# Tile 0's squares to SBUF, tile 7's low parts to GpSimd, and two scans and three loads moved back

## The chip, the cores and the metric

One core of one Trainium2 chip runs the whole kernel. The metric is the device time in microseconds, of which the median of the runs counts. TensorE multiplies matrices, VectorE (DVE in the profile) and ScalarE (ACT) do elementwise work, GpSimd (POOL) does a little of it and issues some transfers, and SyncE (SP) only issues transfers.

## The reference, cut to what matters

Four layers, each added to its input: x (4 sequences of 1024 tokens, 512 features) goes through

```python
x = x + L0(x)   # gelu(x @ fc1) @ [shared fc2, expert fc2 chosen per sequence]
x = x + L1(x)   # a 512x512 matrix chosen per sequence; its result is x2
ctx = ema(x2, tau_ctx)                            # h = alpha*h + b, along the tokens
gated = x2 * sigmoid([x2, ctx] @ Wg + bg)
mod = 0.5 + sigmoid(gelu(x2 @ Wn1 + bn1) @ Wn2 + bn2)           # 4 rows per token
temporal = sum_d blend[d] * ema(gated * mod[d], tau[d])         # 4 scans per feature
out = (gelu(x2 @ Wsoma) * sigmoid(temporal @ Wtemp)) @ Wout
x3 = x2 + layernorm(out) * gamma + beta
x = x3 + L3(x3)  # a 512x512 matrix chosen per sequence
```

All in float32. The layernorm needs the sum over the 512 features of the squares of out.

## The kernel before

A tile is 512 tokens; there are eight (NT), two to a sequence, and LAST is tile 7. Each of the four 128-row chunks of a tile is called c or m. A float32 product is made of three passes over a high part (rounded by ScalarE) and a low part (what is left, a subtraction): hi*hi, hi*lo and lo*hi. So nearly every operand passes through ScalarE (`..._hi`) and then a `low_part` (`..._lo`).

Up to about 760 us the first two layers run. Then comes the third, in rounds r over the tiles: round r makes n1(r) and mo(r) (the modulation rows), gate(r, m), te(r-1, m) (temporal product), l3(r-2, m) (the last layer), ou(r-1, m) (output product), so(r, m) and so_pair(r) (soma products), and ss(r-1) (the sum of squares over partitions). Every engine's order is written out by hand, and semaphores hold the engines together. An engine waits in its own order, so what stands behind a waiting instruction waits too.

The names that matter here:
- `o_of(i, m)` on ScalarE copies the output product out of its bank and squares it; `square_of` says where a square goes, which for tile 0 is the bank itself. `sum_squares(i)` on VectorE adds the four squares to `sumsq`, and counts in s_ssq. `ss(i)` multiplies `sumsq` with ones, and `rows_std(i)` makes 1/std of it.
- x2 of tile 7: `x2_hi`, `x2_lo`, and then its store to x2hl_dram. x2's halves come back as `x2_slot`, by `load_slot(i, c)`; slots 2 and 3 of the next tile are free only when so_pair has used chunks 0 and 1 (s_x2free).
- ctx: `context(t, c)` on VectorE is a scan in x_raw; `ctx_hi(t, c)` (two copies on ScalarE) and `context_lo(t, c)` split it, and `store_ctx(t, h)` stores two chunks.
- `load_xt(i, h)` brings x2 of tile i for `gated_of`. xt of tile 2 lies where x_raw of tile 7 lies (168 KiB), so it waits for all stores of contexts. `load_l3w(b)` brings the last layer's weights of a sequence; every l3(i, m) waits for all four chunks.
- VectorE makes a chunk of temporal out of `gated_of`, and four times `drive_of`, `trace_of` (the scan) and `add_of`; these go by the names traces_a to traces_d, first_traces and first_sum. `temporal_low(i, p)` splits two chunks.

These waits carry the order around the change:

```python
elif i == 2:                                             # load_xt
    on.wait_ge(s_ctxst, 16 * HALVES * NT)
...
on.wait_ge(s_xt[i % 3], 16 * HALVES * (i // 3 + 1))      # gated_of
...
elif i < LAST:                                           # so_pair
    on.wait_ge(s_ssq, SH * i)
...
on.wait_ge(s_h1hi, mo_split_no(i))                       # mo, tiles from 3 on
on.wait_ge(s_h1lo, mo_split_no(i))
```

Of the kernel before, what the change touches and what calls it, by code (L numbers as in the profile page):

```python
# [5 lines left out]
F32 = mybir.dt.float32  # L6
F32R = mybir.dt.float32r
# [36 lines left out]
def build(nc, x, tok16, tok8, small, fc1_w, fc2_w, exp_w, exp_b, l1_w, l1_b, wg, wn1, wsoma, wtemp, wout,  # L44
# [16 lines left out]
    with ctx:  # L61
# [3 lines left out]
        def place(name, kib, shape, dt=F32):  # L65
            return nc.alloc_sbuf_tensor_at(name, [P] + shape, dt, offset=base + int(kib * KIB))
# [84 lines left out]
        x3_hi_late = place("x3_hi_late", 68, [KC, TOK], F32R)  # L151
        sq_late = place("sq_late", 40, [SH, TOK])
        spikes_hi_late = place("spikes_hi_late", 112, [KC, TOK], F32R)
        y_sb = [place("y_sb0", 94, [TOK]), place("y_sb1", 4, [TOK])]

        idx = const("idx", 2 * B, I32)
# [309 lines left out]
        def te_bank(m):  # L466
            return bank[m]
# [44 lines left out]
        def square_of(i, m):  # L512
            if i == LAST:
                return last_squares[m][:, :]
            return te_bank(m)[:, :] if i < LAST - 1 else sq_late[:, m - 1, :]


# [13 lines left out]
        def _(eng):  # L531
# [207 lines left out]
            def load_l3w(b):  # L739
                for c in range(KC):  # L740
                    if b == B - 1 and c == KC - 1:
                        on.wait_ge(s_pe["SO"], KC * LAST)
                    elif b == B - 1:
                        on.wait_ge(s_pe["WG"], KC * LAST + 3)
                    elif b:
                        on.wait_ge(s_pe["L3"], KC * HALVES * b)
                    elif c < 2:
                        for q in range(KC):
                            on.wait_ge(s_hl7[q], 16)
                    else:  # L750
                        on.wait_ge(s_fc2, UNITS)

                        on.wait_ge(s_stlo, STAGED)
                        on.wait_ge(s_pstlo, 16 * len(PARKED))
                        for row in range(2):
                            on.wait_ge(s_hbst[row], 16 * K8 * PAIRS)
                    eng.dma_start(l3w_of_tile(HALVES * b, c)[:, :, :].bitcast(F32), parked("L3", KC * b + c)).then_inc(s_l3w[c], 16)
# [128 lines left out]
            load_slot(2, 0)  # L886
            load_slot(2, 1)
            store_ctx(LAST, 0)
            store_ctx(LAST, 1)
            load_xt(2, 0)  # L890
            load_xt(2, 1)
            load_l3w(0)

            for r in range(1, NT + 2):
                if 1 < r < LAST:
                    load_slot(r + 1, 0)
                    load_slot(r + 1, 1)
                if r >= 2:
                    i = r - 2
                    if r == LAST:  # L900
                        load_l3w(B - 1)
                    for m in range(KC):
                        on.wait_ge(s_y, KC * i + m + 1)
                        source = y_sb[m % 2][:, :] if i < LAST else temporal[:, m, :]
                        eng.dma_start(out[i, :, m, :], source).then_inc(s_out[m % 2], 16)
                    if i + 3 < NT:
                        load_xt(i + 3, 0)
                        load_xt(i + 3, 1)
                    if i % HALVES and i < LAST - 2:
                        load_l3w((i + 1) // HALVES)  # L910
                if r + 1 < NT:
                    for c in range(KC):
                        load_ctx(r + 1, c)
                    load_slot(r + 1, 2)
                    load_slot(r + 1, 3)
            for s in range(2):
                on.wait_ge(s_out[s], 16 * HALVES * NT)
            on.wait_ge(s_x2st, 16 * NT)
# [6 lines left out]
        def _(eng):  # L925
# [60 lines left out]
            for c in range(KC):  # L986
                on.wait_ge(s_fc2, HC * LAST + (9, 11, 12, 13)[c])
                store_hl(LAST - 1, c)
            on.wait_ge(s_made, len(MADE))
            eng.memset(wn2_hl[:, :, :].bitcast(F32), 0.0).then_inc(s_wn2, 1)  # L990
            for i in range(HALVES, NT, HALVES):
                last_columns(i)
        @block.scalar
        def _(eng):
# [479 lines left out]
            ctx_hi(LAST, 1)  # L1474
            wg_tanh(1, 2)
            q_of(1, 3)
            ctx_hi(LAST, 2)
            ctx_hi(LAST, 3)
            wg_tanh(1, 3)
            for m in range(KC):  # L1480
                o_of(0, m)
# [3 lines left out]
            soma_of(1, 1)  # L1485
            for m in range(SH):
                temporal_hi(1, m)
            rows_std(0)
            soma_of(1, 2)
            soma_of(1, 3)  # L1490

            for r in range(2, NT):
                if r == 2:
                    h1_of(r)
                    temporal_hi(r - 1, 3)
                else:
                    temporal_hi(r - 1, 3)
                    h1_of(r)
                    h1_hi_of(r)
                mod_of(r)  # L1500
                modulation_out(r)
                modulation_back(r)
                q_of(r, 0)
                wg_tanh(r, 0)
                te_tanh(r - 1, 0)
                for m in range(HALVES):
                    x3_hi_of(r - 2, m)
                te_tanh(r - 1, 1)
                for m in range(HALVES, KC):
                    x3_hi_of(r - 2, m)  # L1510
                te_tanh(r - 1, 2)
                te_tanh(r - 1, 3)
                for m in range(SH):
                    spikes_hi(r - 1, m)
                q_of(r, 1)
                spikes_hi(r - 1, SH)
                wg_tanh(r, 1)
                q_of(r, 2)
                y_of(r - 2, 0)
                y_of(r - 2, 1)  # L1520
                if r < LAST:
                    y_of(r - 2, 2)
                    y_of(r - 2, 3)
                wg_tanh(r, 2)
                q_of(r, 3)
                o_of(r - 1, 0)
                o_of(r - 1, 1)
                wg_tanh(r, 3)
                o_of(r - 1, 2)
                o_of(r - 1, 3)  # L1530
                if r <= LAST - 1:
                    sumsq_hi(r - 1)
                soma_of(r, 0)
                soma_of(r, 1)
                for m in range(SH):
                    temporal_hi(r, m)
                if r < LAST:
                    rows_std(r - 1)
                soma_of(r, 2)
                soma_of(r, 3)  # L1540
# [31 lines left out]
        def _(eng):  # L1572
# [283 lines left out]
            def so_pair(i):  # L1856
                if i == 0:
                    on.wait_ge(s_x1, KC * NT)
                elif i < LAST:
                    on.wait_ge(s_ssq, SH * i)  # L1860
                else:
                    on.wait_ge(s_sq, KC * i)
                for c in range(KC):
                    for m in (2, 3):
                        mm = so_part(i, m, c)
                        if c == KC - 1:
                            mm.then_inc(s_pe["SO"], 1)
                    if c < 2:
                        mm.then_inc(s_x2free, 1)
# [124 lines left out]
            for r in range(1, NT):  # L1994
                if r > 1:
                    n1(r)
                    gate(r, 0)
                for m in range(SH):
                    te(r - 1, m)
                if r == 1:  # L2000
                    gate(r, 1)
                te(r - 1, SH)
                if r > 1:
                    gate(r, 1)
                gate(r, 2)
                if r > 1:
                    for m in range(KC if r < LAST else 2):
                        l3(r - 2, m)
                gate(r, 3)
                for m in range(KC):  # L2010
                    ou(r - 1, m)
                so(r, 0)
                so(r, 1)
                if r < LAST:
                    ss(r - 1)
                so_pair(r)

            l3(LAST - 2, 2)
            l3(LAST - 2, 3, range(2))
# [20 lines left out]
        def _(eng):  # L2040
# [574 lines left out]
            x2_of(LAST, 3)  # L2615
            traces_a(1, 0)
            spikes(0, 0)
            for c in range(KC):
                x2_lo(LAST, c)
            spikes(0, 1)  # L2620
            first_traces(1, 0)
            context(LAST, 0)
            context(LAST, 1)
            spikes(0, 2)
            gate_sum(1, 1)
            context(LAST, 2)
            context(LAST, 3)
            spikes(0, 3)
            first_sum(1, 0)
            spikes_low(0, 0, 2)  # L2630
            spikes_low(0, 2, 2)
            gate_sum(1, 2)
            traces_c(1, 0)
            context_lo(LAST, 0)
            context_lo(LAST, 1)
            traces_d(1, 0)
            gate_sum(1, 3)
            context_lo(LAST, 2)
            context_lo(LAST, 3)
            traces_a(1, 1)  # L2640
            traces_b(1, 1)
            traces_c(1, 1)
# [12 lines left out]
            low_part(wn2_hl[:, 1, 0:TAUS], wn2_sb, wn2_hl[:, 0, 0:TAUS]).then_inc(s_wn2, 1)  # L2655
            temporal_low(1, 0)
            temporal_low(1, 2)
            for r in range(2, NT):
                if r > 2:
                    h1_low(r)  # L2660
# [2 lines left out]
                gate_sum(r, 0)  # L2663
                for m in range(KC):
                    x3_of(r - 2, m)
                traces_a(r, 0)
                spikes(r - 1, 0)
                spikes(r - 1, 1)
                x3_low(r - 2, 0, 2)
                x3_low(r - 2, 2, 2)  # L2670
                spikes(r - 1, 2)
                first_traces(r, 0)
                spikes(r - 1, 3)
# [118 lines left out]
```

## Time and profile before

| | |
|---|---|
| median of 3 runs | 1296.02 us (1295.71 to 1296.36) |
| the profiled execution | 1295.54 us, its span 1293.7 us |
| mean granted clock of TensorE | 0.997 |
| TensorE matmuls busy | 1274.4 us, 99% |
| VectorE busy | 1066.6 us, 82% |
| ScalarE busy | 718.7 us, 56% |
| GpSimd busy | 66.8 us, 5% |
| DMA | 262.62 MB, mean 203 GB/s |

Times of rows are in microseconds from the start of the span. The busy share is a mean over the whole kernel; what an edit is worth is read at its place. The span is from the first to the last instruction of the profiled execution, and the time of that execution is 1.8 us more.

### The profile page before, as it was taken

The numbers are of one execution on the slowest core, as the hardware profiler recorded it, in microseconds if no ns is written. First come the engines' busy times: TensorE is split into PE (matmuls) and PEld (weight loads), VectorE is DVE, ScalarE is ACT, GpSimd is POOL, SyncE is SP. The second block draws the span as 40 slices with busy tenths as digits, with TensorE's granted clock in tenths as the row PEclk, the third lists the DMA queues.
The fourth block names the chain that finished last, engine by engine and source line by source line (L and its number), as shares of the span: only waits on it lengthen the run. The fifth ranks groups of instructions, "written<-read, shape, count | busy, mean of one in ns | idle before, by whom it ended". The sixth has DMA issues, their size and how long they took to land.

```text
span 1293.7 us, 17500 instructions
## 1 busy us (share of the span) xinstructions
PE 1274.4 (99%) x6109; PEld 1068.1 (83%) x6109; DVE 1066.6 (82%) x1698; ACT 718.7 (56%) x1369; POOL 66.8 (5%) x102
## 2 busy tenths in 40 slices
PE   9999999999999999999999999899999999999998
PEld 7788888888888888888887888778888888888867
DVE  7877777887786987777875899999898989898974
ACT  6576465776565875566763353443636363636254
POOL 0010000000000000000000000002000210021000
PEclk9999999999999999999999999999999999999999
DMA  8357653658744657645558797966465646663301
GB/s 293 98 171 238 192 174 122 220 174 270 216 170 145 238 167 266 225 141 178 188 206 277 297 329 289 345 227 231 160 240 215 227 164 232 224 222 137 130 17 65
DMA packets 114286, 262.62 MB, mean 203 GB/s; under 512 B 10344, under 2 KB 32872, under 8 KB 109080
## 3 DMA queue, kind: packets, MB, share of 16 engines
q1 hardware_dynamic: 94336, 183.27, 41.6%
q10 hardware_dynamic: 15032, 62.45, 13.7%
q0 software_dynamic: 4832, 15.79, 3.2%
q8 instruction: 49, 0.80, 0.3%
q14 instruction: 37, 0.30, 0.1%
HBM read 181.19 MB, written 80.28 MB: 202 GB/s over the span
## 4 chain that ended last, share of the span: by engine, by line
PE 81%; DVE 13%; DMA 2%; ACT 2%; issue 2%; ACTq 0%; DVEq 0%
PE bank L1577 27%; PE bank L1578 27%; PE bank L1579 26%; DVE drive L2289 4%; DVE drive L2278 2%; DVE temporal L2305 1%; DMA x_slot<-x2hl_dram 1%; DMA hb_in<-hb_dram 1%; DVE x_hl L2044 1%; DVE h_hl L2044 1%; DVE w_hl L2044 1%; DVE t_lo L2044 0%; DVE x_raw L2244 0%; DVE gated L2265 0%; DMA x_raw<-in_x 0%
## 5 line engine op out<-in xcount | busy, mean ns | idle before, releaser
L1577 PE MATMUL bank<-h_hl,w_hl 128*128 128x512 f32 x512 | 199.6, 390 | 0.0
L1578 PE MATMUL bank<-h_hl,w_hl 128*128 128x512 f32 x512 | 199.3, 389 | 0.0
L1579 PE MATMUL bank<-h_hl,w_hl 128*128 128x512 f32 x512 | 199.2, 389 | 0.0
L1577 PE MATMUL bank<-t_hi,sp_hl 128*128 128x512 f32 x448 | 175.2, 391 | 3.5 <-DVE t_lo L2044 1.1
L1578 PE MATMUL bank<-t_lo,sp_hl 128*128 128x512 f32 x448 | 174.4, 389 | 0.0
L1579 PE MATMUL bank<-t_hi,sp_hl 128*128 128x512 f32 x448 | 174.4, 389 | 0.0
L1577 PEld LDWEIGHTS bank<-h_hl,w_hl 128*128 128x128 f32 x512 | 96.1, 188 | 21.1 <-issue 1.3
L1579 PEld LDWEIGHTS bank<-h_hl,w_hl 128*128 128x128 f32 x512 | 96.1, 188 | 20.0
L1578 PEld LDWEIGHTS bank<-h_hl,w_hl 128*128 128x128 f32 x512 | 96.2, 188 | 19.6
L1577 PEld LDWEIGHTS bank<-t_hi,sp_hl 128*128 128x128 f32 x448 | 84.1, 188 | 24.3 <-issue 1.8
L1579 PEld LDWEIGHTS bank<-t_hi,sp_hl 128*128 128x128 f32 x448 | 84.1, 188 | 17.5
L1578 PEld LDWEIGHTS bank<-t_lo,sp_hl 128*128 128x128 f32 x448 | 84.1, 188 | 17.1
L2278 DVE SCALAR_TENSOR_TENSOR drive<-gated,small_sb,mod_t 128x512 f32<-128x512 f32 x128 | 92.6, 744 | 2.7
L2044 DVE TENSOR_TENSOR w_hl<-w_raw,w_hl 128x512 fp32r<-128x512 f32 x128 | 86.4, 683 | 4.4 <-ACT w_hl L1035 3.9
L1102 ACT ACTIVATE h_hl<-hb_in 128x512 fp32r<-128x512 f32 x64 | 40.1, 627 | 82.2 <-DMA hb_in<-hb_dram 63.3
L1035 ACT ACTIVATE w_hl<-w_raw 128x512 fp32r<-128x512 f32 x128 | 78.3, 619 | 6.4 <-PE bank L1579 6.3
L2289 DVE TENSOR_TENSOR_SCAN drive<-alpha,trace_last,drive 128x512 f32<-128x512 f32 x64 | 80.2, 1274 | 0.5
L2044 DVE TENSOR_TENSOR h_hl<-hb_in,h_hl 128x512 fp32r<-128x512 f32 x64 | 43.8, 684 | 42.9 <-ACT h_hl L1102 42.9
L2289 DVE TENSOR_TENSOR_SCAN drive<-alpha,drive 128x512 f32<-128x512 f32 x64 | 76.7, 1214 | 0.5
L1577 PE MATMUL bank<-x_slot,wg_hl 128*128 128x256 f32 x256 | 73.0, 285 | 0.0
L1578 PE MATMUL bank<-x_slot,wg_hl 128*128 128x256 f32 x256 | 73.0, 285 | 0.0
L1579 PE MATMUL bank<-x_slot,wg_hl 128*128 128x256 f32 x256 | 73.0, 285 | 0.0
(229 smaller groups left out, 3026.8 us busy)
## 6 DMA issues: line engine op xcount, KB each, us to landing
wg_hl<-wg_dram ACTq DMA_DIRECT2D x24, 1536.0 KB, 7.8
fc_raw<-in_fc_w SPq DMA_DIRECT2D x32, 512.0 KB, 4.2
hb_dram<-hb_out SPq DMA_DIRECT2D x64, 256.0 KB, 2.2
hb_in<-hb_dram ACTq DMA_DIRECT2D x64, 256.0 KB, 4.2
x2hl_dram<-x_hl POOLq DMA_DIRECT2D x28, 512.0 KB, 5.6
x_slot<-x2hl_dram SPq DMA_DIRECT2D x26, 512.0 KB, 5.8
wg_hl<-wg_dram SPq DMA_DIRECT2D x8, 1536.0 KB, 8.5
stage<-in_l_w SPq DMA_DIRECT2D x32, 256.0 KB, 3.4
```

The source lines that it names most:

```text
L1035: eng.activation(w2_hl[v % 3][:, 0, :, :], w2_raw[:, j, :, :], ACT.Copy).then_inc(s_w2hi, 1)
L1102: eng.activation(h_hl[v % 4][:, 0, :], hb_in[v % 4][:, :], ACT.Copy).then_inc(s_hhi, 1)
L1577: eng.matmul(ps, w_hi, x_hi, start=first, stop=False, skip_group_check=resumed)
L1578: eng.matmul(ps, w_hi, x_lo, start=False, stop=False, skip_group_check=resumed)
L1579: return eng.matmul(ps, w_lo, x_hi, start=False, stop=final, skip_group_check=resumed)
L2044: return eng.tensor_tensor(lo, raw, hi.bitcast(F32), ALU.subtract)
L2278: eng.scalar_tensor_tensor(drive[d % 2][:, :], gated[:, :], blend_sb[:, TAUS * c + d:TAUS * c + d + 1], mod_t[:, d, :], ALU.mult, ALU.mult ...
L2289: eng.tensor_tensor_scan(traced, alpha[:, 1 + d:2 + d].to_broadcast([P, TOK]), traced, start, ALU.mult, ALU.add).then_inc(s_trace, 1)
L2305: eng.tensor_tensor(temporal[:, c, :], drive[d % 2][:, :], temporal[:, c, :] if d > 1 else drive[0][:, :], ALU.add).then_inc(s_add, 1)
```

## The change

It has five parts. The squares 1 to 3 of tile 0 go to three places in SBUF (200, 202 and 90 KiB) instead of their banks; chunks 2 and 3 of the last layer's weights, which lie over them, wait for the sum. With the banks free sooner, so_pair(1) waits for the squares alone, and ss(0) goes behind it. The subtractions x2_lo and context_lo of tile 7 go from VectorE to GpSimd. The scans of tile 7's chunks 2 and 3 go behind tile 1's temporal_low, their ctx_hi on ScalarE behind the modulation rows of round 2. In SyncE's queue the second store of tile 7's context, and with it the loads of xt(2) and of the last layer's weights, go behind the loads of ctx(2) and slots (2, 2) and (2, 3). On ScalarE rows_std(0) goes behind two somas, and on VectorE traces_a(2, 0) behind two spikes and the low parts of x3.

```diff
+        sq_first = [place(f"sq_first{m}", at, [TOK]) for m, at in enumerate((200, 202, 90))]
...
             if i == LAST:
                 return last_squares[m][:, :]
+            if i == 0:
+                return sq_first[m - 1][:, :]
...
                         on.wait_ge(s_pstlo, 16 * len(PARKED))
+
+                        on.wait_ge(s_ssq, SH)
...
             store_ctx(LAST, 0)
-            store_ctx(LAST, 1)
-            load_xt(2, 0)
-            load_xt(2, 1)
-            load_l3w(0)
...
                     load_slot(r + 1, 2)
                     load_slot(r + 1, 3)
+                if r == 1:
+                    store_ctx(LAST, 1)
+                    load_xt(2, 0)
+                    load_xt(2, 1)
+                    load_l3w(0)
...
+            for c in range(KC):
+                on.wait_ge(s_x2hi, KC * LAST + c + 1)
+                eng.tensor_tensor(halves(x_hl[:, 1, c, :]), even_odd(x_raw[LAST % 2][:, c, :]),
+                                  halves(x_hl[:, 0, c, :]).bitcast(F32), ALU.subtract).then_inc(s_x2lo, 1)
             on.wait_ge(s_made, len(MADE))
             eng.memset(wn2_hl[:, :, :].bitcast(F32), 0.0).then_inc(s_wn2, 1)
+            for c in range(KC):
+                on.wait_ge(s_ctxhi, KC * LAST + c + 1)
+                z = x_raw[LAST % 2][:, c, :]
+                eng.tensor_tensor(z[:, 0:PAIR].bitcast(F32R), z[:, 0:PAIR], z[:, PAIR:], ALU.subtract
+                                  ).then_inc(s_ctxlo, 1)
...
             q_of(1, 3)
-            ctx_hi(LAST, 2)
-            ctx_hi(LAST, 3)
             wg_tanh(1, 3)
...
-            rows_std(0)
             soma_of(1, 2)
             soma_of(1, 3)
+            rows_std(0)
...
                 modulation_back(r)
+                if r == 2:
+                    ctx_hi(LAST, 2)
+                    ctx_hi(LAST, 3)
                 q_of(r, 0)
...
             def so_pair(i):
-                elif i < LAST:
+                elif 1 < i < LAST:
                     on.wait_ge(s_ssq, SH * i)
...
-                if r < LAST:
+                if 1 < r < LAST:
                     ss(r - 1)
                 so_pair(r)
+                if r == 1:
+                    ss(0)
...
             spikes(0, 0)
-            for c in range(KC):
-                x2_lo(LAST, c)
             spikes(0, 1)
...
-            context(LAST, 2)
-            context(LAST, 3)
             spikes(0, 3)
...
-            context_lo(LAST, 0)
-            context_lo(LAST, 1)
             traces_d(1, 0)
             gate_sum(1, 3)
-            context_lo(LAST, 2)
-            context_lo(LAST, 3)
             traces_a(1, 1)
...
             temporal_low(1, 0)
             temporal_low(1, 2)
+            context(LAST, 2)
+            context(LAST, 3)
...
-                traces_a(r, 0)
+                if r > 2:
+                    traces_a(r, 0)
                 spikes(r - 1, 0)
                 spikes(r - 1, 1)
                 x3_low(r - 2, 0, 2)
                 x3_low(r - 2, 2, 2)
+                if r == 2:
+                    traces_a(r, 0)
```

## Rows read from the trace of the kernel before

**Rows 1.** The page's busy times (us, share of the span, instructions).

```profile
PE 1274.4 (99%) x6109; PEld 1068.1 (83%) x6109; DVE 1066.6 (82%) x1698; ACT 718.7 (56%) x1369; POOL 66.8 (5%) x102
```

**Rows 2.** TensorE's waits, 800 to 1000 us: total, times, longest.

```profile
PE bank L1885 <- DVE sumsq L2359: 3.9, 1, 3.9
PE bank L1577 <- DMA x_slot<-x2hl_dram: 2.7, 1, 2.7
```

**Rows 3.** One window: length, busy time by engine, PEclk, DMA share, GB/s.

```profile
852.00:854.00 2.00, 2.00 (x9) 1.71 (x8) 2.00 (x3) 0.73 (x1) 0.00 (x0) 0.53 0.30 119
```

**Rows 4.** SyncE's timeline: start, length, line, transfer, count.

```profile
834.58 0.79 SPq L702 DMA_DIRECT2D xt<-x_dram  x2
...
842.76 0.32 SPq L728 DMA_DIRECT2D x_slot<-x2hl_dram  x1
```

**Rows 5.** DMA issues at 912.6, 652.4, all, 834.6, 891.1, 837.1 us: count, KB, us to landing.

```profile
x_slot<-x2hl_dram SPq DMA_DIRECT2D x1, 512.0 KB, 4.5
...
ctx_dram<-x_raw SPq DMA_DIRECT2D x2, 512.0 KB, 3.4
...
ctx_dram<-x_raw SPq DMA_DIRECT2D x16, 512.0 KB, 6.1
...
xt<-x_dram SPq DMA_DIRECT2D x2, 512.0 KB, 4.7
...
xt<-x_dram SPq DMA_DIRECT2D x2, 512.0 KB, 9.0
...
l3w_hl<-l3w_dram SPq DMA_DIRECT2D x2, 512.0 KB, 9.3
```

**Rows 6.** VectorE's timeline: start, length of all, instruction, count, wait before it.

```profile
810.27 0.66 DVE L2346 SCALAR_TENSOR_TENSOR soma<-bank,soma 128x512 f32<-128x512 f32 x1
...
817.62 0.75 DVE L2044 TENSOR_TENSOR x_raw<-x_raw 128x256 fp32r<-128x256 f32 x2
...
836.33 2.25 DVE L2359 TENSOR_TENSOR sumsq<-bank,sumsq 128x512 f32<-128x512 f32 x3
...
854.86 2.35 DVE L2044 TENSOR_TENSOR temporal_lo<-temporal,ts_hi 128x1024 fp32r<-128x1024 f32 x2
...
864.40 0.68 DVE L2265 SCALAR_TENSOR_TENSOR gated<-bank,xt 128x512 f32<-128x512 f32 x1
...
877.30 0.69 DVE L2257 TENSOR_TENSOR bank<-bank,q_sb 128x512 f32<-128x512 f32 x1
...
906.51 0.69 DVE L2359 TENSOR_TENSOR sumsq<-bank,sumsq 128x512 f32<-128x512 f32 x1 [1.46 <-ACT bank L1251]
...
920.80 0.69 DVE L2044 TENSOR_TENSOR h_lo<-h,h_hi 128x512 fp32r<-128x512 f32 x1 [0.48 <-ACT h_hi L1149]
```

**Rows 7.** ScalarE's timeline, from 808 to 861 us.

```profile
808.61 0.65 ACT L1204 ACTIVATE bank<-bank,small_sb 128x512 f32<-128x512 f32 x1
...
833.68 0.58 ACT L1251 ACTIVATE bank<-bank 128x512 f32<-128x512 f32 x1
...
845.14 1.28 ACT L1264 ACT_TABLE_LOAD   x1
...
856.54 0.68 ACT L1153 ACTIVATE mod_row<-bank,small_sb 4x512 f32<-4x512 f32 x1 [1.00 <-PE bank L1735]
...
860.29 0.38 ACT L1177 ACTIVATE q_sb<-bank 128x256 f32<-128x256 f32 x1 [2.32 <-DMA mod_dram<-mod_row]
```

**Rows 8.** TensorE's timeline: so(1, 1)'s last, gate(2, 0), l3(0, 0), mo(3).

```profile
834.42 0.39 PE L1579 MATMUL bank<-x_slot,wsoma_hl 128*128 128x512 f32 x1
...
852.79 0.41 PE L1577 MATMUL bank<-x_slot,wg_hl 128*128 128x256 f32 x1
...
878.94 0.40 PE L1577 MATMUL bank<-x_hi,l3w_hl 128*128 128x512 f32 x1
...
922.05 0.39 PE L1577 MATMUL bank<-h_hi,wn_hl 128*64 128x512 f32 x1
```

**Rows 9.** GpSimd's copies (min/median/max ns) and its affine_select (busy us, mean ns).

```profile
L971 POOL COPY trace_last<-drive x48: 182/707/1035, 871.8 to 1177.3; 128x1 f32<-128x1 f32 x48
...
L932 POOL TENSOR_SCALAR_AFFINE_SELECT ident<-ident 128x128 f32<-128x128 f32 x1 | 0.3, 282 | 0.2 <-POOL ident L930 0.2
```

## The prediction

> **What bounds the kernel now.** I read the page first: TensorE is busy in 1274.4 of 1293.7 us [rows 1], so all that any edit can win is what TensorE waits, plus what its clock takes back. The waits of TensorE between 800 and 1000 us come second. Nearly all of it is two waits: 3.9 us for tile 0's sum of squares and 2.7 us for a half of x2 on its way from DRAM [rows 2]. The windows give the third part: from 852 us the granted clock is 0.53 [rows 3], which is the lower of the two levels (1.2 of 2.4 GHz) after the second wait; a 256-column matmul then costs 0.21 instead of 0.12 us, about 1.6 us in all, and some 0.8 us more after the first wait. Tile 1's first two soma products end at 834.65, and gate(2, 0) begins at 852.79 [rows 8]; the work between them is 9.15 us (24 + 12 matmuls of 0.227 and 0.95 for ss), so 9.0 us need not be there. Then I went to what releases each wait: SyncE's queue [rows 4], the landing times [rows 5], VectorE [rows 6] and ScalarE [rows 7], and followed them as far as the next round, because VectorE hardly idles there: from 862 to 921 us it waits only 1.46 us ahead of 906.5 and 0.48 ahead of 920.8 [rows 6].
>
> **Removed waits.** With ss(0) behind so_pair(1), TensorE goes on at 834.65: the pair needs only the fourth square, which ends at 833.68 + 0.58 = 834.3 [rows 7]. Writing the squares to SBUF instead of a bank I cost at nothing; 0.1 us each, which no row suggests, would just be hidden. The pair's 24 matmuls of 0.227 end at 840.1. The sum of squares ended at 836.33 + 2.25 = 838.6 [rows 6] and comes sooner below, so the 3.9 us go. The pair's sixth matmul now ends at 836.0, not 842.7, and so does SyncE's wait for a free slot [rows 4]. In front of that load nothing is queued any more (the 1 MB of xt and the 2 MB of l3w stood there), so 4.5 us as in the next round [rows 5] is nearer than its 8.0 here: landed at 840.7, wanted at 840.1 + 1.0 (ss) + 1.4 = 842.4. The 2.7 us go too. n1(2) ends at 843.8.
>
> **VectorE.** It loses x2_low (2.4 us), two scans (2.4) and four context_low (two pairs of 0.67 [rows 6]); 6.1 us. Most of that turns into a wait: spikes(0, 3) cannot start before te_tanh(0, 3) ends at 808.61 + 0.66 = 809.3 [rows 7], 0.95 before its 810.27 [rows 6]. Behind it only the two pairs are gone, so it is 0.95 + 1.34 = 2.3 ahead; I take 2.1 for a little friction with GpSimd. The sum of squares then ends at 836.5, and temporal_low(1, ·), 854.86 + 2.35, ends at 855.0 instead of 857.15.
>
> **GpSimd.** The trace shows no 128x512 subtraction on it. Near rows: affine_select of 128x128 in 0.28 us, times four 1.1, and a copy of one column that can last 1.0 instead of 0.2 [rows 9]; so 1.1 to 2.1 us each. I take 1.2, near the row of like width, and 0.6 to 0.75 for 256 columns. x2's four then end at about 803 and the store of x2 is issued only at 807.2 anyway: 2.1 us each, done by 804.5, would still be hidden. The first two context_lo end at 815, before their store can matter.
>
> **What TensorE finds next.** ScalarE: temporal_hi(1, 2) at 842.4, then 0.63, 1.3 for two somas, 0.7 for rows_std and 0.7 for h1 with a table load of 1.28 [rows 7] ahead of each of the last two: h1 of tile 2 is there at 848.3. TensorE is at mo(2) at 845.2: 3.1 us of a new wait, and probably a low clock behind it. te(1, 0) needs temporal_low(1, 0), at 854.0; before, it began at 859.4. So of 9.0 us, 5.4 are left; four te and two gates later gate(2, 2) ends at 873.5 instead of 878.94 [rows 8].
>
> **The loads behind the moved scans.** xt of tile 2 lies where x_raw of tile 7 lies: load_xt(2) waits until all of tile 7's context is stored (s_ctxst), and load_l3w(0) is queued behind it. Before, xt was issued at 834.58 [rows 4], l3w right behind. Now: the two scans on VectorE 855.0 to 857.4; on ScalarE ctx_hi(7, 2) and (7, 3) stand behind mod_of(2) and the way of its rows to DRAM and back, where q_of(2, 0) stood. From mod_of to q_of it was 860.29 - 856.54 = 3.75 [rows 7]; mod_of now begins at 853.4, behind temporal_hi(1, 3), so they begin at 857.2, and four copies of 0.4 end at 858.8; context_lo(7, 3) on GpSimd ends at 859.5 to 860.5; store at 860.2. The store takes 3.4 us alone and 6.1 as the median [rows 5]; wg(10), 1.5 MB, runs beside it, so 5.0: 865.3. The two halves of xt take 4.7 us with nothing beside, 9.0 with a wg started 1 us before [rows 5]; here that wg is nearly done: 6.0 after the second issue at 865.8. So xt(2) is there at X = 871.7 (ends: 868.4 and 876).
>
> gated_of(2, 0) waits for it; before it ran at 864.40 [rows 6]. The diff puts two spikes and two x3_low (3.47 us) ahead of it, but they are done by 867. From gated_of to gate_sum(2, 1) it was 877.30 - 864.40 = 12.90 us [rows 6], now 12.90 - 3.47 = 9.43: gate_sum(2, 1) at X + 9.43, late by L = X - 867.87 = 3.8 us. Behind it VectorE has no gap until 906.5, then 1.46 and 0.48 [rows 6]. h1_low(3) ended at 921.45 and mo(3) began at 922.05 [rows 8], 0.6 of slack. So mo(3) moves by L - 1.46 - 0.48 - 0.6 = X - 870.4 = **+1.3 us**. Behind mo(3) hang the modulation rows, q and the gates of tile 3, where VectorE had a gap of over 3 us; so the shift is neither won back nor grows.
>
> The other branch: the last l3w needed 9.3 us from issue [rows 5]; issued at 866.3 to 867.9, with the rest of a wg and two slot loads about, all four are there at 877.5 to 878.5. TensorE is ready at 873.5, waits 4 us or so, and pays up to 1.7 us of low clock: l3(0, 2) at -0.4 to +1.2 against before. y_of(0, 0), behind gate_sum(2, 1) on ScalarE, gives about the same. The VectorE branch is the later one, and sets.
>
> **Sum.** 9.0 us won by 853, 5.4 by the first te, about 1 at l3(0, 0), -1.3 at mo(3): 1295.54 + 1.3 = 1296.8 for the profiled execution; the median of the three runs is 0.5 above that execution, so **1297.3**. The reordered SyncE queue otherwise costs nothing: ctx_slot is loaded sooner, slots (3, 0) and (3, 1) wanted at 916 are issued at 869, the output stores start after 882. GpSimd's last_columns(2) stands behind context_lo(7, 3) at 860.5, its first scan after 872.
>
> **Rivals.** (1) *Forecast*: the late xt(2) eats the gain, -2.6 to +2.6 us; 0.48. (2) *Faster*: store and load take no more than they do on an empty queue, or less (rows say 3.4 + 4.7, X = 868.4, which gives -2.0); at X of 866.9 VectorE never waits and L is -1.0. mo(3) is then 3.5 us sooner: 1292.5. Against it: a wg is always in flight there. With what I may have missed in my own chain, 0.20. (3) *Slower by late transfers*: store 6.1 and xt 8 give X = 874.8, mo(3) +4.4: 1300.4. It decides from X = 873.0 on. The low clock after a wait of 4 us speaks for it on TensorE's side; 0.19. (4) *Slower by the lock*: GpSimd's copies of one column take 182 ns at best, 707 in the middle and 1035 at most [rows 9], so something beside them holds them up; the same may hold VectorE up. If each GpSimd subtraction stops VectorE for its length, 4 x 1.1 us less a gap of 2.8 before spikes(0, 3), and 2 x 0.6 behind it, make 2.8 us where I put 0.2: temporal_low, and X with it, 2.6 later, +3.9: 1299.9; 0.13. The Trainium skill, SBUF — State Buffer ("Who interferes with whom"), has that rule: a VectorE instruction with two SBUF inputs and a GpSimd one that reads SBUF exclude each other for the whole instruction. The row agrees for GpSimd's side; none shows VectorE held.
>
> **How the numbers follow.** 0.2% is 2.6 us, about what can be told from no change. Faster: (2), 0.20. Same: (1), 0.48. Slower: (3) and (4), 0.32. The range goes down to a little under rival 2, 1292.0, and up past rival 3 but not to the far end of X (876 gives +5.6), 1301.5.
>
> **What would show it.** No wait at ss(0) nor at n1(2) near 840; mo(2) near 848 after some 3 us of wait; te(1, 0) near 854; VectorE idle for about 4 us ahead of gated_of(2, 0), released by xt's load, at 871.7; TensorE waiting for l3w ahead of l3(0, 0) near 878; a lower clock once or twice between 845 and 882; mo(3) near 923. If gated_of(2, 0) doesn't wait, the forecast is wrong and the kernel is some 3 us faster; if GpSimd's pieces take 2 us and VectorE's scans beside them grow beyond 1.3, it is rival 4.

## The result, and the profile after

The changed kernel takes **1300.2 us** (median of 7 runs, 1299.4 to 1302.8) where the kernel before takes 1295.4 (7 runs, 1294.2 to 1296.4): ratio 1.004, 95% interval 1.003 to 1.005. It is 4.8 us slower, more than the 2.6 us that can be told from no change. The range of 1292.0 to 1301.5 holds it; the likeliest case, +1.3 us, is not what came. What came has the price of rival 3, 1300.4.

The profiled execution took 1301.53 us. One caution for every table below: it already ran 1.47 us behind the kernel before when tile 1's soma products began (830.68 against 829.21 us), and the executions of one kernel differ by some 3 us, so positions in the span are compared after taking this offset off. I call that *aligned*.

The page, answering to [rows 1]: TensorE's work has grown by 0.8 us, its span by 5.9.

```profile
span 1299.6 us, 17499 instructions
...
PE 1275.2 (98%) x6109; PEld 1067.8 (82%) x6109; DVE 1067.9 (82%) x1690; ACT 718.7 (55%) x1369; POOL 78.6 (6%) x110
```

TensorE's waits from 800 to 1000 us, answering to [rows 2]:

```profile
PE bank L1595 <- DMA l3w_hl<-l3w_dram: 5.3, 1, 5.3
PE bank L1753 <- ACT h L1160: 3.4, 1, 3.4
...
PE bank L1595 <- DVE h_lo L2064: 0.8, 1, 0.8
PE bank L1595 <- DVE temporal_lo L2064: 0.2, 1, 0.2
```

Both old waits are gone and two new ones add up to more: 3.4 us for h of tile 2, 5.3 us for the last layer's weights. TensorE's timeline shows where they stand; brackets hold the wait and its releaser.

```profile
841.57 1.02 PE L1903 MATMUL bank<-sumsq,ones 128*128 128x512 f32 x2
842.02 0.80 PE L1595 MATMUL bank<-x_slot,wn_hl 128*128 128x512 f32 x1
...
850.16 1.33 PE L1753 MATMUL bank<-h,small_sb 128*4 128x512 f32 x2 [3.38 <-ACT h L1160]
...
855.96 0.47 PE L1595 MATMUL bank<-ts_hi,wtemp_hl 128*128 128x512 f32 x1 [0.20 <-DVE temporal_lo L2064]
...
881.11 0.77 PE L1595 MATMUL bank<-x_hi,l3w_hl 128*128 128x512 f32 x1 [5.33 <-DMA l3w_hl<-l3w_dram]
```

ss(0) and n1(2) follow the soma products without a gap. Aligned, te(1, 0) starts at 854.5 against 859.4, so 4.9 us are in hand; l3(0, 0) starts at 879.6 against 878.9 [rows 8], so 0.7 us is owed; mo(3), at 927.36, starts 3.8 us late. The whole loss lies between 855 and 927.

VectorE's timeline tells the rest of it, answering to [rows 6]:

```profile
854.60 2.35 DVE L2064 TENSOR_TENSOR temporal_lo<-temporal,ts_hi 128x1024 fp32r<-128x1024 f32 x2
856.87 2.46 DVE L2264 TENSOR_TENSOR_SCAN x_raw<-alpha,g_last,x_raw 128x512 f32<-128x512 f32 x2
...
867.29 2.34 DVE L2064 TENSOR_TENSOR x_lo<-xt,x_hi 128x1024 fp32r<-128x1024 f32 x2
875.48 0.69 DVE L2285 SCALAR_TENSOR_TENSOR gated<-bank,xt 128x512 f32<-128x512 f32 x1 [5.85 <-DMA xt<-x_dram]
...
884.93 0.69 DVE L2277 TENSOR_TENSOR bank<-bank,q_sb 128x512 f32<-128x512 f32 x1
...
911.22 2.27 DVE L2379 TENSOR_TENSOR sumsq<-bank,sumsq 128x512 f32<-128x512 f32 x3
```

The engine that had hardly a gap up to 906 us stands still for 5.85 us, waiting for xt of tile 2. The gap ahead of the sum of squares (1.46 us in [rows 6]) is used up. SyncE's timeline, and then the transfers' time to landing (count, KB, us), say why xt is late:

```profile
862.40 0.32 SPq L693 DMA_DIRECT2D ctx_dram<-x_raw  x1
869.58 0.80 SPq L706 DMA_DIRECT2D xt<-x_dram  x2
870.55 2.32 SPq L763 DMA_DIRECT2D l3w_hl<-l3w_dram  x4
```

```profile
ctx_dram<-x_raw SPq DMA_DIRECT2D x1, 512.0 KB, 7.2
...
xt<-x_dram SPq DMA_DIRECT2D x2, 512.0 KB, 4.7
...
l3w_hl<-l3w_dram SPq DMA_DIRECT2D x4, 512.0 KB, 7.5
```

The store waits for the moved scans, takes 7.2 us, and the loads of xt and of the weights wait for the store. xt was issued at 834.58 before [rows 4], at 869.58 now. Windows of the same stretch (length, busy time by engine, granted clock, DMA share, GB/s), answering to [rows 3]:

```profile
850.00:855.00 5.00, 4.84 (x22) 3.67 (x23) 4.93 (x8) 0.47 (x2) 0.00 (x0) 0.66 0.00 0
875.00:880.00 5.00, 0.78 (x7) 0.58 (x5) 4.48 (x6) 1.27 (x3) 0.58 (x1) 0.81 1.05 402
880.00:885.00 5.00, 3.89 (x9) 3.12 (x10) 4.86 (x8) 0.63 (x1) 1.26 (x3) 0.51 1.01 372
```

The granted clock falls behind the first wait and already within the second: 0.66 and 0.81 are means over both levels, 0.51 is the lower one (1.2 of 2.4 GHz). From l3(0, 0) to gate(2, 3) it is 12.76 us instead of 10.91: 1.85 us for the clock.

### The profile page after: what moved, and what is told of

Read it like the earlier page. It is cut to its first block and busy times, and to the rows that moved or that the text cites. A ratio compares the mean times of both kernels' runs of the same rounds, so it can differ in the third digit from the quotient of the medians.

```text
span 1299.6 us, 17499 instructions
## 1 busy us (share of the span) xinstructions
PE 1275.2 (98%) x6109; PEld 1067.8 (82%) x6109; DVE 1067.9 (82%) x1690; ACT 718.7 (55%) x1369; POOL 78.6 (6%) x110
## 5 line engine op out<-in xcount | busy, mean ns | idle before, releaser
L1205 ACT ACTIVATE bank<-bank,small_sb 128x512 f32<-128x512 f32 x32 | 21.2, 661 | 98.3 <-DVE bank L2277 98.3
L1595 PE MATMUL bank<-x_slot,wg_hl 128*128 128x256 f32 x256 | 72.5, 283 | 0.0
L1596 PE MATMUL bank<-x_slot,wg_hl 128*128 128x256 f32 x256 | 72.4, 283 | 0.0
```

The lines of the kernel that those rows point to most:

```text
L1205: eng.activation(ps[:, :], ps[:, :], ACT.Tanh, bias=bg_sb[:, m:m + 1], scale=0.5).then_inc(s_wgt, 1)
L1595: eng.matmul(ps, w_hi, x_hi, start=first, stop=False, skip_group_check=resumed)
L1596: eng.matmul(ps, w_hi, x_lo, start=False, stop=False, skip_group_check=resumed)
```

## The experiments

Eight kernels, each with 5 to 11 runs beside 15 to 21 runs of the kernel before on the same chip. "After" is the changed kernel, "before" the one without it; names are those of the kernel section above.

| kernel | median us | ratio to before, 95% | mo(3), aligned, against before |
|---|---|---|---|
| changed kernel | 1300.2 | 1.004 (1.003 to 1.005) | +3.8 |
| 1 scans back | 1293.56 | 0.9991 (0.9982 to 1.0000) | -2.3 |
| 2 low parts back | 1299.65 | 1.0039 (1.0025 to 1.0053) | +3.9 |
| 3 weights first | 1300.57 | 1.0042 (1.0029 to 1.0056) | +4.5 |
| 4 squares and queue | 1293.37 | 0.9990 (0.9981 to 0.9999) | -2.7 |
| 5 squares alone | 1295.43 | 1.0001 (0.9992 to 1.0010) | -0.9 |
| 6 scans moved alone | 1300.15 | 1.0038 (1.0025 to 1.0052) | +4.0 |
| 7 contexts on GpSimd | 1293.51 | 0.9986 (0.9977 to 0.9995) | -2.7 |
| 8 queue alone | 1296.36 | 1.0010 (1.0001 to 1.0019) | -0.4 |

The last column is the start of mo(3) counted from the start of tile 1's soma products, less the same distance before (922.05 - 829.21 = 92.84 us).

**1. The moved scans back.** From the changed kernel:

```diff
             gate_sum(1, 1)
+            context(LAST, 2)
+            context(LAST, 3)
             spikes(0, 3)
...
             temporal_low(1, 2)
-            context(LAST, 2)
-            context(LAST, 3)
```

with ctx_hi(7, 2) and (7, 3) and traces_a(2, 0) back in their old places too.

> The changed kernel with the two scans of tile 7's chunks 2 and 3, their ctx_hi and traces_a(2, 0) back where they stood before; squares, ss order, GpSimd's low parts and SyncE's new order stay. Theory (late loads: xt(2) and the weights come too late because the store waits for the moved scans): the store is issued near 839, xt(2) is there by 846, neither VectorE nor TensorE waits for either, and the total falls to 1292.5 (1291 to 1294.5). Rival (GpSimd's lock on VectorE is what costs): the lock on x2's four pieces and on context_lo is still there, so the total stays at 1297 to 1300.

Measured: 1293.56 us, within what the first theory gave, and 6.6 us below the changed kernel's median (6.2 us when each is set against the kernel before on its own chip: +4.8 and -1.4). TensorE's waits have only one entry over 1 us, and VectorE's row at gate_sum(2, 0) has no wait worth the name:

```profile
PE bank L1752 <- ACT h L1160: 5.3, 1, 5.3
```

```profile
859.96 0.70 DVE L2276 TENSOR_TENSOR bank<-bank,q_sb 128x512 f32<-128x512 f32 x1 [0.16 <-ACT q_sb L1195]
```

What follows: with the scans back, xt and the weights are never late, and the loss is gone (0.9991, 0.9982 to 1.0000). The GpSimd parts are all still in it, so the lock rival's 1297 to 1300 did not come.

**2. The low parts back on VectorE.** From the changed kernel: the two loops on GpSimd go, x2_lo(LAST, 0 to 3) stands behind spikes(0, 0) again, and context_lo(LAST, 0) to (LAST, 3) run on VectorE, the last two behind the moved scans.

```diff
-            for c in range(KC):
-                on.wait_ge(s_x2hi, KC * LAST + c + 1)
...
             spikes(0, 0)
+            for c in range(KC):
+                x2_lo(LAST, c)
...
+                if r == 2:
+                    context_lo(LAST, 2)
+                    context_lo(LAST, 3)
                 gate_sum(r, 0)
```

> The changed kernel with x2_lo and context_lo of tile 7 back on VectorE (the last two behind z_of of round 2, since the scans stay moved). Late loads: the store is issued 0 to 1.5 us sooner, everything behind it is hardly changed: 1299.3 (1298 to 1300.5). Lock rival: the 4.8 us come back, 1296 or less.

Measured: 1299.65 us. The lock, rival 4, falls as the cause of the loss: with no GpSimd arithmetic in the kernel the loss is the same, and so is the wait.

```profile
873.81 0.69 DVE L2276 SCALAR_TENSOR_TENSOR gated<-bank,xt 128x512 f32<-128x512 f32 x1 [5.87 <-DMA xt<-x_dram]
```

**3. The weights ahead of the store.** From the changed kernel:

```diff
                 if r == 1:
+                    load_l3w(0)
                     store_ctx(LAST, 1)
                     load_xt(2, 0)
                     load_xt(2, 1)
-                    load_l3w(0)
```

> The changed kernel with load_l3w(0) ahead of store_ctx(7, 1) and load_xt(2) in SyncE's queue. TensorE no longer waits 5.3 us ahead of l3(0, 0) nor pays for the low clock behind it. If VectorE's late gated_of(2, 0) sets the end, as the prediction had it, mo(3) stays where it is within 1 us: 1299.5. If TensorE's wait for the weights and its low clock set it, 2 to 4 us come back: 1297.

Measured: 1300.57 us. TensorE's 5.3 us wait for the weights is gone, and nothing is won: another wait stands behind it.

```profile
PE bank L1595 <- ACT y_sb L1301: 6.1, 1, 6.1
PE bank L1753 <- ACT h L1160: 3.6, 1, 3.6
```

l3(0, 2) needs y_of(0, 0), which stands behind gate_sum(2, 1) on ScalarE's path, and that hangs on xt. So the weights alone are worth nothing: with them in time, TensorE stands still for xt by another way. Reading only TensorE's waits would have named the weights. That VectorE's branch is the later one at mo(3) is shown by the changed kernel's own wait there, 0.8 us for h_lo. In experiment 3 mo(3) begins without a wait, 0.7 us later still: aligned, l3(0, 2) starts at 886.0 and not at 887.0, but it starts at the low clock behind its wait of 6.1 us, and gate(2, 3) starts at 894.0 and not at 892.4.

**4. Squares and queue only.** From the kernel before, these edits and no other:

```diff
+        sq_first = [place(f"sq_first{m}", at, [TOK]) for m, at in enumerate((200, 202, 90))]
...
+            if i == 0:
+                return sq_first[m - 1][:, :]
...
+                        on.wait_ge(s_ssq, SH)
...
             store_ctx(LAST, 0)
-            store_ctx(LAST, 1)
-            load_xt(2, 0)
-            load_xt(2, 1)
-            load_l3w(0)
...
+                if r == 1:
+                    store_ctx(LAST, 1)
+                    load_xt(2, 0)
+                    load_xt(2, 1)
+                    load_l3w(0)
...
-                elif i < LAST:
+                elif 1 < i < LAST:
...
-                if r < LAST:
+                if 1 < r < LAST:
                     ss(r - 1)
                 so_pair(r)
+                if r == 1:
+                    ss(0)
```

> The kernel before with only the squares in SBUF, ss(0) behind so_pair(1) and SyncE's new order; scans, low parts, rows_std and traces_a(2, 0) stay as before. Late loads: both waits at 835 to 851 go, the store is issued at 838, nothing waits for xt(2): te(1, 0) at 856 instead of 859.4, then VectorE sets: 1292.5 (1291.5 to 1294). Rival (VectorE alone is the bound there, so TensorE's waits before it are worth nothing): 1295.4, no change.

Measured: 1293.37 us, 0.1% (1.6 us) faster than before, the interval just clear of no change. It is level with experiments 1 and 7 (1293.56 and 1293.51), and it leaves out everything that the change did on GpSimd and with the scans. The rival of an unchanged 1295.4 falls, narrowly. TensorE's waits, then three rows of VectorE's timeline, and behind them a row of the kernel before, for the first of the three:

```profile
PE bank L1740 <- ACT h L1148: 5.1, 1, 5.1
```

```profile
859.83 0.70 DVE L2264 TENSOR_TENSOR bank<-bank,q_sb 128x512 f32<-128x512 f32 x1 [0.17 <-ACT q_sb L1183]
...
905.25 0.69 DVE L2051 TENSOR_TENSOR sumsq_lo<-sumsq,ts_hi 128x512 fp32r<-128x512 f32 x1
...
917.93 0.69 DVE L2051 TENSOR_TENSOR h_lo<-h,h_hi 128x512 fp32r<-128x512 f32 x1 [0.26 <-ACT h_hi L1154]
```

```profile
861.14 0.70 DVE L2257 TENSOR_TENSOR bank<-bank,q_sb 128x512 f32<-128x512 f32 x1 [1.28 <-ACT q_sb L1178]
```

Three gaps of VectorE have closed or nearly so: 1.28 us ahead of gate_sum(2, 0) became 0.17, and the 1.46 and 0.48 us of [rows 6] are nothing and 0.26. 1.1 + 1.5 + 0.2 = 2.8 us, and mo(3) is 2.7 sooner. So what the faster TensorE won here is about VectorE's idle time, and little of that is left. TensorE's own waits fell only from 6.6 to 5.1 + 0.4 us.

**5. Squares alone.** As 4, with SyncE's queue as before:

```diff
+            store_ctx(LAST, 1)
+            load_xt(2, 0)
+            load_xt(2, 1)
+            load_l3w(0)
...
-                if r == 1:
-                    store_ctx(LAST, 1)
-                    load_xt(2, 0)
-                    load_xt(2, 1)
-                    load_l3w(0)
```

> The kernel before with only the squares in SBUF and ss(0) behind so_pair(1); SyncE's order stays. The 3.9 us wait goes, but slot (2, 2) is still queued behind xt, the weights and ctx: issued at 840, landed about 848, wanted at 842.4, so 5 to 6 us of wait at n1(2) in place of 2.7. te(1, 0) then begins about 856.5, and from there on it is as with the queue's new order: 1293.5 (1292.5 to 1295). If the queue's order is what wins, 1295.

Measured: 1295.43 us, nothing won (1.0001, 0.9992 to 1.0010); mo(3) is 0.9 us sooner. TensorE takes its time up in one wait:

```profile
PE bank L1581 <- DMA x_slot<-x2hl_dram: 7.6, 1, 7.6
```

The load of slot (2, 2) was issued at 842.58 (aligned 841.9, before 842.76), hardly sooner than before, because SyncE was still issuing the 3 MB and the context loads queued ahead of it (the four weight loads took 3.8 us to issue, not the 2.2 of before), and it needed 8.2 us to land. I had expected it at 840. Removing the sum's wait was worth nothing by itself: the wait for the slot took its place.

**6. The scans moved alone.** From the kernel before: the scans, ctx_hi, the last two context_lo (on VectorE) and traces_a(2, 0) moved as in the change, with the new queue they need; no squares in SBUF and no GpSimd arithmetic.

```diff
-            context(LAST, 2)
-            context(LAST, 3)
             spikes(0, 3)
...
             temporal_low(1, 2)
+            context(LAST, 2)
+            context(LAST, 3)
...
+                if r == 2:
+                    ctx_hi(LAST, 2)
+                    ctx_hi(LAST, 3)
                 q_of(r, 0)
...
+                if r == 2:
+                    context_lo(LAST, 2)
+                    context_lo(LAST, 3)
                 gate_sum(r, 0)
```

> The kernel before with only the moved scans, their ctx_hi and context_lo and traces_a(2, 0) behind them, and SyncE's new order (without it the slots would wait too); squares, ss and VectorE's low parts as before. Late loads: xt(2) and the weights come as late as in the changed kernel, VectorE waits some 6 us and TensorE some 5: 1299.3 (1298 to 1301), as slow as the whole change though it holds no GpSimd arithmetic. Rival (the lock, or the squares' new order, causes a part of the loss): under 1297.5.

Measured: 1300.15 us, the whole loss. ctx_hi and traces_a(2, 0) moved with the scans in this experiment and in the first, but what the two rows below wait for is again the late transfers, as in the changed kernel:

```profile
PE bank L1579 <- DMA l3w_hl<-l3w_dram: 5.4, 1, 5.4
```

```profile
874.68 0.69 DVE L2267 SCALAR_TENSOR_TENSOR gated<-bank,xt 128x512 f32<-128x512 f32 x1 [6.09 <-DMA xt<-x_dram]
```

**7. Experiment 4 with the four context_lo on GpSimd.**

```diff
+            for c in range(KC):
+                on.wait_ge(s_ctxhi, KC * LAST + c + 1)
+                z = x_raw[LAST % 2][:, c, :]
+                eng.tensor_tensor(z[:, 0:PAIR].bitcast(F32R), z[:, 0:PAIR], z[:, PAIR:], ALU.subtract
+                                  ).then_inc(s_ctxlo, 1)
...
-            context_lo(LAST, 0)
-            context_lo(LAST, 1)
...
-            context_lo(LAST, 2)
-            context_lo(LAST, 3)
```

> The fourth experiment's kernel with tile 7's four context_lo on GpSimd instead of VectorE: 1.34 us less work for VectorE, which sets te(1, 0) there. If GpSimd's reads hold VectorE up for about their overlap, as its longer rows in the changed kernel say, most of it is given back: temporal_low(1, ·) under 0.7 us earlier and the time within 0.7 us of the fourth's. If offloading is free, 1.3 us earlier in both.

Measured: 1293.51 us against 1293.37 of experiment 4. VectorE gives 1.3 us of work away and has temporal_low at the same place: 854.86 in 4 and 854.91 here, both aligned. That is what was expected if GpSimd holds VectorE up, and not the 1.3 us of a free offload. GpSimd's timeline, and VectorE's row beside the first pair:

```profile
813.30 2.87 POOL L999 TENSOR_TENSOR x_raw<-x_raw 128x256 fp32r<-128x256 f32 x2 [56.82 <-ACT x_raw L1145]
818.40 2.42 POOL L999 TENSOR_TENSOR x_raw<-x_raw 128x256 fp32r<-128x256 f32 x2 [2.23 <-ACT x_raw L1145]
```

```profile
812.69 2.88 DVE L2056 TENSOR_TENSOR spikes_lo<-soma,ts_hi 128x1024 fp32r<-128x1024 f32 x2
```

The same two spikes take 2.35 us in experiment 4. Beside GpSimd's second pair stand a scan and an addition that are longer too:

```profile
818.53 1.76 DVE L2301 TENSOR_TENSOR_SCAN drive<-alpha,trace_last,drive 128x512 f32<-128x512 f32 x1
820.33 1.05 DVE L2317 TENSOR_TENSOR temporal<-drive,temporal 128x512 f32<-128x512 f32 x1
```

In 4 they take 1.28 and 0.69. 0.53 + 0.48 + 0.36 = 1.4 us: all that was given away came back in three instructions.

**8. The queue alone.** From the kernel before, only the SyncE edits of experiment 4:

```diff
-            store_ctx(LAST, 1)
-            load_xt(2, 0)
-            load_xt(2, 1)
-            load_l3w(0)
...
+                if r == 1:
+                    store_ctx(LAST, 1)
+                    load_xt(2, 0)
+                    load_xt(2, 1)
+                    load_l3w(0)
```

> The kernel before with one edit: in SyncE's queue the second store of tile 7's context, the two loads of xt(2) and the four of the last layer's weights go behind the loads of ctx(2) and of slots (2, 2) and (2, 3), as in e4; squares stay in their banks and ss(0) stays ahead of so_pair(1). Theory (the queue's order is worth all that e4 won, the squares nothing): the 2.7 us wait for x2's half goes, the 3.9 us wait for the sum of squares stays or shrinks to 2.4 as in e6; TensorE then still waits only once, for h at mo(2) or not at all, te(1, 0) begins at 856.0 to 857.0 and the median is 1293.5 (1292.8 to 1294.2). Rival (both are needed, because with ss(0) ahead of the pair slot (2, 2) comes free 2.5 us or more later than in e4, and q(2, 0) with it): n1(2)'s rows wait about 2 us for the slot, and the median is 1294.6 to 1295.5.

Measured: 1296.36 us, not faster than before and outside both ranges. By mo(3) this kernel is 0.4 us ahead, so what makes its median 1.2 us longer than that of the kernel before beside it does not lie in this stretch, and was not followed. Both edits are needed, as the rival said, but not by its mechanism: te(1, 0) begins at 856.3 aligned, as the theory had it, slot (2, 2) lands after 3.9 us and n1(2) does not wait. VectorE waits instead, for q(2, 0); its row and ScalarE's:

```profile
864.13 0.70 DVE L2258 TENSOR_TENSOR bank<-bank,q_sb 128x512 f32<-128x512 f32 x1 [3.17 <-ACT q_sb L1179]
```

```profile
857.99 0.27 ACTq L1163 DMA_DIRECT2D mod_dram<-mod_row  x1
862.42 0.81 ACTq L1169 DMA_DIRECT2D mod_t<-mod_dram  x2
```

ss(0) ahead of the pair frees the slot late (843.75), so xt, the weights and the slots follow from 851.0 to 855.2, and the 8 KB of modulation rows, stored at 857.99, travel beside them: 4.4 us until they can be read back. In experiment 4 the same loads went out at 843.3 to 847.5 and had nearly all landed by then; there it is 1.4 us:

```profile
856.69 0.27 ACTq L1167 DMA_DIRECT2D mod_dram<-mod_row  x1
858.12 0.81 ACTq L1173 DMA_DIRECT2D mod_t<-mod_dram  x2
```

That these loads are what held the small store up is inferred from the two timelines; no run took them away.

## Why the prediction came out as it did

**Removed waits.** Right. Both went, and ss(0) and n1(2) follow the pair. Experiments 5 and 8 add what the prediction did not say: neither edit has a value of its own in the time.

**VectorE.** 2.1 us ahead at temporal_low was forecast, 1.7 came (854.60, aligned 853.1, against 854.86). The friction that was taken as 0.2 us is 0.4: one drive beside the first pair of context_lo takes 1.16 us and not 0.73. The difference to experiment 2 is 0.3 us. There x2_lo and the first pair of context_lo, 3.2 us (2.49 + 0.67), stand on VectorE ahead of temporal_low; moving them to GpSimd bought that much.

**GpSimd.** Undersized, all beside a busy VectorE: 1.5 us for each 128x512 piece and 1.2 to 1.6 for 128x256, where I took 1.2 and 0.6 to 0.75.

```profile
797.55 6.03 POOL L999 TENSOR_TENSOR x_hl<-x_raw,x_hl 128x512 fp32r<-128x512 f32 x4 [40.21 <-ACT x_hl L1140]
...
814.41 3.19 POOL L1006 TENSOR_TENSOR x_raw<-x_raw 128x256 fp32r<-128x256 f32 x2 [10.69 <-ACT x_raw L1152]
859.86 2.51 POOL L1006 TENSOR_TENSOR x_raw<-x_raw 128x256 fp32r<-128x256 f32 x2 [42.26 <-ACT x_raw L1152]
```

**TensorE's next waits.** Right: h at mo(2) after 3.4 us (3.1 forecast), mo(2) aligned at 848.7 (848.3), te(1, 0) at 854.5 (854.0).

**The loads behind the moved scans: the step that was mis-sized.** The formula held and its X did not. X was taken as 871.7 and measured 874.0 aligned (874.1 in experiment 2, 874.2 in 6). The formula X - 870.4 then gives +3.6 to +3.8; mo(3) moved by +3.8, +3.9 and +4.0. Three terms make the 2.3 us. The store was issued at 860.9 aligned, not 860.2 (+0.7); with the low parts on VectorE it is later still, 861.4 and 861.5. It took 7.2 us, not 5.0 (+2.2); experiments 2 and 6 both have 6.9. And from its landing to gated_of(2, 0) it was 5.9 us, not 6.4, because xt needs the 4.7 us that [rows 5] give for an empty queue (-0.5). The store is the term that counts. I had set it between the 3.4 of a quiet queue and the median of 6.1, with wg(10), a 1.5 MB load of the gates' weights, beside it. The trace says how long that was: wg(10) was issued at 860.16 behind the two halves of mod_t (858.04, 4.4 us) and took 8.5, so it ran until 868.7, beside nearly the whole of a store that lasted from 862.4 to 869.6. In the four runs where a wg load is in flight beside this store (the changed kernel, 2, 3, 6) it takes 6.9 to 7.2 us, in the four where only slot loads are (1, 4, 7, 8) 5.0 to 5.4. No run takes the wg load away, so that it is the cause is inferred.

**The other branch.** TensorE waited 5.3 us for the weights, not 4, and paid 1.85 us of low clock (1.7 forecast). l3(0, 2) came 2.5 us later than before, where -0.4 to +1.2 was forecast. TensorE still had to wait 0.8 us for h_lo at mo(3), so VectorE's branch is the later one, as forecast, but not by much.

**The sum.** Forecast +1.3, measured +4.8 by the medians and +3.8 at mo(3). 2.3 of the 3.5 us between them are X. Of the other 1.2 us, 0.2 lie ahead of mo(3) and some 0.6 behind it: the profiled span is 5.9 us longer, 4.4 aligned, where the prediction had nothing behind mo(3). The rest is between medians and one profile; the runs do not split it.

**The rivals.** Rival 2 needed a quiet queue, which xt found (4.7 us) and the store did not. Rival 3's numbers, store 6.1 and xt 8, were each off (7.2 and 4.7), but their sum gave X = 874.8, close to 874.0; that its price, 1300.4, is so near the median is partly luck. Rival 4 has a true mechanism and the wrong place. VectorE is held up where GpSimd works: the first pair of drive takes 3.50 us, 1.41 in the kernel before, and the pair of scans 3.59 against 2.45.

```profile
797.64 3.50 DVE L2298 SCALAR_TENSOR_TENSOR drive<-gated,small_sb,mod_t 128x512 f32<-128x512 f32 x2
801.06 1.28 DVE L2366 SCALAR_TENSOR_TENSOR soma<-bank,soma 128x512 f32<-128x512 f32 x2
802.26 3.59 DVE L2309 TENSOR_TENSOR_SCAN drive<-alpha,trace_last,drive 128x512 f32<-128x512 f32 x2
...
810.85 0.69 DVE L2366 SCALAR_TENSOR_TENSOR soma<-bank,soma 128x512 f32<-128x512 f32 x1 [1.47 <-ACT bank L1221]
...
815.80 1.27 DVE L2309 TENSOR_TENSOR_SCAN drive<-alpha,trace_last,drive 128x512 f32<-128x512 f32 x1
816.99 1.16 DVE L2298 SCALAR_TENSOR_TENSOR drive<-gated,small_sb,mod_t 128x512 f32<-128x512 f32 x1
...
859.24 3.68 DVE L2389 SCALAR_TENSOR_TENSOR o_sb<-o_sb,small_sb,rstd 128x512 f32<-128x512 f32 x4
```

2.1 + 1.1 = 3.2 us, about what rival 4's own numbers give: 4 x 1.1 less the 1.28 us of the two soma between them, which read a bank and are not longer beside GpSimd. There it costs nothing: x2_lo's 2.49 us and a wait of 0.67 us, which experiment 2 has in the same stretch, are gone, and the stretch ends in a wait for ScalarE anyway, 1.47 us ahead of 810.85 (1.30 in experiment 2). Behind that wait the pair of context_lo saves 0.67 us and a drive takes 0.4 more, which leaves the 0.3 us at temporal_low. The four o_sb (3.68 against 2.73) come after temporal_low. So the offload cost nothing net and, as experiment 2 shows, bought nothing in the time. The Trainium skill, SBUF — State Buffer ("Who interferes with whom"), states that a VectorE instruction with two SBUF inputs and a GpSimd one that reads SBUF exclude each other for their whole length. These rows agree: the drives and scans, with both inputs in SBUF, lose 3.2 us beside 6.0 us of GpSimd, and the two soma with an input in a bank lose nothing. Not each such instruction is the one that is held up: the scan at 815.80, beside context_lo's first pair, takes its usual 1.27 us.

## What to carry to other kernels

When a step is moved, follow every load that waits for its output's place, not only the output: here two scans of 1.2 us each, moved back by 48 us, took 3 MB of loads with them, and that cost over 6 us against the version without the move. Size a transfer on the critical path by what else is in flight in its own stretch, not by the median of its kind. And try the parts of a compound change alone and in pairs: here two were worth 1.6 us only together, one cost all, and the offload to GpSimd was worth nothing.

## What the runs showed of the hardware

- A GpSimd subtraction slows VectorE's instructions beside it whose inputs both lie in SBUF, if not each of them (two drives 3.50 us against 1.41, one scan 1.27 as alone), and not those with an input in a bank (two soma 1.28, as before). Moving 1.3 us (experiment 7) or 3.2 us (the change against experiment 2) of VectorE's work to GpSimd brought temporal_low 0 and 0.3 us forward.
- A 512 KB store took 5.0 to 5.4 us behind slot loads (experiments 1, 4, 7, 8), and 6.9 to 7.2 us beside a load of 1.5 MB (the changed kernel, 2, 3, 6); the two 512 KB loads of xt right after it took 4.7 in experiment 4 and in the changed kernel.
- An 8 KB store to DRAM came back after 1.4 us in one queue state and after 4.4 us in another (experiment 8).
- Issuing the same four loads took SyncE 2.2 to 2.3 us in most runs, 2.7 in experiment 3 and 3.8 us in experiment 5.
